# The same steps in a new written order on all five engines of a one-core macaron block with routed experts

## What is computed

```python
x = x + 0.5 * quantized_ffn(layernorm(x))          # int8 activations and weights
x = x + rg_lru_layer(layernorm(x))                 # conv, gated scan, then a gelu MLP of 512
x = x + 0.5 * quantized_ffn(layernorm(x))
x = x + 0.5 * moe(layernorm(x))                    # shared expert + top 2 of 8, inner width 256
x = x + gated_linear_attention(layernorm(x))       # state 128x128 for each of 16 sequences
x = x + 0.5 * moe(layernorm(x))                    # same weights again
```

## Time and profile before

| | |
|---|---|
| runs | 701.73, 701.86, 702.95 us; median 701.86 |
| profiled execution, its span | 703.3 us |
| PE / PEld busy | 616.8 us (88%) / 487.0 us (69%) |
| DVE busy | 487.2 us (69%) |
| ACT busy | 398.0 us (57%) |
| POOL busy | 387.9 us (55%) |
| moved by DMA | 100.99 MB, mean 144 GB/s |

### The profile page before, as it was taken

The page is one execution under the profiler, slowest core; times in us unless marked ns, Lnnn a source line. Parts: engine busy times, 40 slices in busy tenths (PEclk is TensorE's granted clock), DMA queues, the critical chain, the costliest instruction groups (busy, mean ns, idle before and its releaser), DMA issues.

```text
span 703.3 us, 14597 instructions
## 1 busy us (share of the span) xinstructions
PE 616.8 (88%) x4232; PEld 487.0 (69%) x4232; DVE 487.2 (69%) x1730; ACT 398.0 (57%) x1036; POOL 387.9 (55%) x416
## 2 busy tenths in 40 slices
PE   1478999999799989899986998899999999987971
PEld 1234565566566888788885886779878998776970
DVE  6986777878889867554625996878865874546334
ACT  3477887999686454554445556464665446343530
POOL 4425434435747787767653413651865764766642
PEclk9699999999999999999999999999999999999996
DMA  7998000000042366577668010214324545566886
GB/s 263 410 411 342 1 0 1 1 1 20 31 107 61 95 179 179 168 214 223 189 200 286 22 66 11 63 46 117 89 73 134 157 115 161 166 197 175 251 302 214
DMA packets 60126, 100.99 MB, mean 144 GB/s; under 512 B 10288, under 2 KB 28592, under 8 KB 59792
## 3 DMA queue, kind: packets, MB, share of 16 engines
q1 hardware_dynamic: 50832, 81.52, 37.7%
q0 software_dynamic: 8640, 17.84, 7.1%
q10 hardware_dynamic: 576, 0.69, 0.3%
HBM read 61.79 MB, written 38.23 MB: 142 GB/s over the span
## 4 chain that ended last, share of the span: by engine, by line
PE 59%; DVE 10%; ACT 9%; issue 7%; DMA 6%; POOL 5%; SPq 4%; POOLq 0%; ACTq 0%; DVEq 0%
PE bank L1071 14%; PE bank L1048 7%; PE bank L1282 4%; PE bank L934 3%; DMA tin<-rows_by_expert 3%; PE bank L959 3%; PE bank L308 3%; PE bank L945 3%; PE bank L510 3%; PE bank L663 3%; PE bank L313 3%; POOL rows_by_expert L830 2%; PE bank L677 2%; PE bank L1054 2%; PE bank L692 2%
## 5 line engine op out<-in xcount | busy, mean ns | idle before, releaser
L830 POOL DMA_INDIRECT rows_by_expert<-xx,sidx x128 | 126.3, 987 | 71.7 <-DVE xx L809 35.8
L1071 PE MATMUL bank<-tint,twt 128*128 128x128 f32 x1136 | 150.7, 278 | 10.9 <-DVE thidt L1109 5.7
L1071 PEld LDWEIGHTS bank<-tint,twt 128*128 128x128 f32 x1136 | 138.6, 192 | 26.3 <-issue 13.6
L1109 DVE TENSOR_TENSOR thidt<-tsil,bank 128x256 f32<-128x256 f32 x142 | 58.9, 419 | 98.6 <-ACT tsil L1087 86.6
L1120 POOL DMA_INDIRECT rows_done<-tout,tin x98 | 95.4, 974 | 52.4 <-ACT tout L1095 28.3
L1087 ACT ACTIVATE tsil<-bank 128x256 f32<-128x256 f32 x142 | 54.4, 384 | 82.1 <-PE bank L1071 80.4
L1048 PE MATMUL bank<-e_dn,thidt 128*128 x568 | 89.8, 283 | 7.3 <-issue 3.5
L1048 PEld LDWEIGHTS bank<-e_dn,thidt 128*128 128x128 f32 x568 | 76.4, 193 | 19.4 <-issue 18.8
L1095 ACT ACTIVATE tout<-bank,tin 128x128 f32<-128x128 f32 x142 | 51.5, 367 | 35.1 <-PE bank L1054 33.7
L1120 POOL DMA_INDIRECT rows_done<-tout,tdst x44 | 43.8, 996 | 30.1 <-issue 11.8
L1080 ACT ACTIVATE tint<-bank 128x128 f32<-128x128 f32 x142 | 38.2, 275 | 37.1 <-PE bank L1054 36.8
(11 more groups left out here) (271 smaller groups left out, 1363.9 us busy)
## 6 DMA issues: line engine op xcount, KB each, us to landing
twt<-moe_gu SPq DMA_DIRECT2D x142, 256.0 KB
rows_by_expert<-tout SPq DMA_DIRECT2D x25, 715.0 KB, 19.6
tin<-rows_by_expert SPq DMA_DIRECT2D x142, 65.0 KB
hid<-rows_done SPq DMA_DIRECT2D x12, 512.0 KB, 4.8
x<-x_in SPq DMA_DIRECT2D x8, 256.0 KB, 4.1
rows_by_expert<-xx,sidx POOLq DMA_INDIRECT x128
out<-x SPq DMA_DIRECT2D x8, 256.0 KB, 3.5
rows_done<-tout,tin POOLq DMA_INDIRECT x98, 3.0
```

Of the source, the lines that this page charges most:

```text
L830: pool.indirect_dma_start(out=rows_by_expert, out_offset=bass.IndirectOffsetOnAxis(ap=sidx[h][:, k:k + 1], axis=0), in_=xx[h][:, r, t, :], ...
L1071: m = pe.matmul(bank[UP_BANKS[p][j]][:, c * P:(c + 1) * P], weights[:, c * P:(c + 1) * P], tint[g % TURNS][:, :], start=True, stop=True)
L1109: dve.tensor_tensor(thidt[g % TURNS][:, :, :].rearrange("p j c -> p (j c)"), tsil[g % TURNS][:, :], bank[UP_BANKS[p][j]][:, INNER:2 * INNE ...
```

## The change

Steps, semaphores, waits inside the steps and buffers are the same. Each of the five lists holds the same steps as before, in another order. Counted by index in their list, 246 of 315 steps of SyncE, 504 of 637 of VectorE, 158 of 285 of GpSimd, 564 of 711 of TensorE and 622 of 751 of ScalarE stand at another place, by at most 7, 41, 22, 19 and 26 places. The order of some is turned around between neighbours; loops are written anew for it. The parts that matter here:

```diff
@@ -1476,277 +1476,216 @@
         @block.sync
         def _(sp_):
             k_loads_sync(sp_)
-            for j in range(0, 2):
+            for j in range(0, 9):
                 t_load_sync(sp_, 0, j)
...
+            t_load_sync(sp_, 0, 63)
+            for j in range(61, 63):
+                t_weights_sync(sp_, 0, j)
             t_stored_sync(sp_, 0, 0)
             c_fetch_sync(sp_, 0, 0)
             c_fetch_sync(sp_, 1, 0)
-            t_load_sync(sp_, 0, 66)
-            for j in range(63, 65):
+            for j in range(64, 67):
+                t_load_sync(sp_, 0, j)
+            for j in range(63, 67):
                 t_weights_sync(sp_, 0, j)
-            for j in range(67, 70):
+            t_load_sync(sp_, 0, 67)
+            c_fetch_sync(sp_, 2, 0)
+            t_weights_sync(sp_, 0, 67)
+            for j in range(68, 70):
                 t_load_sync(sp_, 0, j)
-            c_fetch_sync(sp_, 2, 0)
-            t_weights_sync(sp_, 0, 65)
             c_fetch_sync(sp_, 3, 0)
-            for j in range(66, 70):
+            c_fetch_sync(sp_, 4, 0)
+            for j in range(68, 70):
                 t_weights_sync(sp_, 0, j)
-            c_fetch_sync(sp_, 4, 0)
+            t_load_sync(sp_, 0, 70)
             t_weights_sync(sp_, 0, 70)
-            t_load_sync(sp_, 0, 70)
...
+            for j in range(66, 69):
+                t_load_sync(sp_, 1, j)
+            t_weights_sync(sp_, 1, 66)
             t_stored_sync(sp_, 1, 0)
             c_fetch_sync(sp_, 0, 1)
-            t_load_sync(sp_, 1, 67)
-            for j in range(65, 67):
+            t_weights_sync(sp_, 1, 67)
+            for j in range(69, 71):
+                t_load_sync(sp_, 1, j)
+            for j in range(68, 70):
                 t_weights_sync(sp_, 1, j)
-            t_load_sync(sp_, 1, 68)
             c_fetch_sync(sp_, 1, 1)
-            t_load_sync(sp_, 1, 69)
-            for j in range(67, 69):
-                t_weights_sync(sp_, 1, j)
-            t_load_sync(sp_, 1, 70)
             c_fetch_sync(sp_, 2, 1)
-            t_weights_sync(sp_, 1, 69)
-            c_fetch_sync(sp_, 3, 1)
             t_weights_sync(sp_, 1, 70)
             o_store_sync(sp_, 0)
+            o_store_sync(sp_, 1)
+            c_fetch_sync(sp_, 3, 1)
             c_fetch_sync(sp_, 4, 1)
-            o_store_sync(sp_, 1)
-            o_store_sync(sp_, 2)
             c_fetch_sync(sp_, 5, 1)
             t_stored_sync(sp_, 1, 6)
             c_fetch_sync(sp_, 6, 1)
+            o_store_sync(sp_, 2)
+            o_store_sync(sp_, 3)
             t_stored_sync(sp_, 1, 7)
             c_fetch_sync(sp_, 7, 1)
-            o_store_sync(sp_, 3)
...
 
         @block.vector
         def _(dve):
+            q_stats_vector(dve, 0, 0)
             q_limits_vector(dve, 0, 0)
-            q_stats_vector(dve, 0, 0)
             q_mom1_vector(dve, 0)
+            q_limits_vector(dve, 1, 0)
             k_first_vector(dve)
+            q_stats_vector(dve, 1, 0)
+            q_mom1_vector(dve, 1)
             q_par1_vector(dve, 0)
-            q_stats_vector(dve, 1, 0)
             q_scale_vector(dve, 0, 0)
-            q_limits_vector(dve, 1, 0)
             q_whole_vector(dve, 0, 0)
-            q_mom1_vector(dve, 1)
             q_par1_vector(dve, 1)
             q_scale_vector(dve, 1, 0)
+            q_whole_vector(dve, 1, 0)
             q_out_vector(dve, 0, 0)
-            q_whole_vector(dve, 1, 0)
-            q_limits_vector(dve, 2, 0)
+            q_stats_vector(dve, 3, 0)
+            q_stats_vector(dve, 2, 0)
             f_stats_vector(dve, 0)
-            k_weights_vector(dve)
             q_out_vector(dve, 1, 0)
             f_stats_vector(dve, 1)
             f_mom_vector(dve, 0)
+            k_weights_vector(dve)
+            k_decay_vector(dve)
+            q_limits_vector(dve, 2, 0)
             q_limits_vector(dve, 3, 0)
-            q_stats_vector(dve, 2, 0)
-            q_stats_vector(dve, 3, 0)
             q_mom_vector(dve, 1, 0)
             q_limits_vector(dve, 4, 0)
             q_par_vector(dve, 1, 0)
             q_scale_vector(dve, 2, 0)
+            q_scale_vector(dve, 3, 0)
             q_whole_vector(dve, 2, 0)
+            q_whole_vector(dve, 3, 0)
+            q_stats_vector(dve, 4, 0)
             q_limits_vector(dve, 5, 0)
-            q_stats_vector(dve, 4, 0)
             q_stats_vector(dve, 5, 0)
-            q_limits_vector(dve, 6, 0)
             q_mom_vector(dve, 2, 0)
-            k_decay_vector(dve)
-            q_stats_vector(dve, 6, 0)
-            q_scale_vector(dve, 3, 0)
-            q_whole_vector(dve, 3, 0)
-            q_limits_vector(dve, 7, 0)
             q_out_vector(dve, 2, 0)
+            f_stats_vector(dve, 2)
             q_par_vector(dve, 2, 0)
+            q_scale_vector(dve, 4, 0)
             f_left_vector(dve, 0)
+            q_whole_vector(dve, 4, 0)
             f_ix_vector(dve, 0)
-            f_stats_vector(dve, 2)
-            q_scale_vector(dve, 4, 0)
-            f_ix_vector(dve, 1)
+            q_out_vector(dve, 3, 0)
             f_left_vector(dve, 1)
-            q_out_vector(dve, 3, 0)
             f_stats_vector(dve, 3)
             f_mom_vector(dve, 1)
             f_scan_vector(dve, 0)
             f_hy_vector(dve, 0)
             f_apply_vector(dve, 0)
...
+            q_whole_vector(dve, 5, 1)
+            q_stats_vector(dve, 6, 1)
+            r_slot_vector(dve, 2, 0)
+            q_out_vector(dve, 4, 1)
             e_add_vector(dve, 1, 0)
-            m_add_vector(dve, 6)
-            r_slot_vector(dve, 2, 0)
-            q_whole_vector(dve, 5, 1)
-            q_out_vector(dve, 4, 1)
...
             x_hid_vector(dve, 0, 4)
+            q_par_vector(dve, 3, 1)
+            q_scale_vector(dve, 6, 1)
+            q_whole_vector(dve, 6, 1)
+            x_hid_vector(dve, 0, 5)
             r_bias_vector(dve, 4, 0)
+            q_scale_vector(dve, 7, 1)
             e_hid_vector(dve, 3, 0, 0)
             r_rank_vector(dve, 4, 0)
-            x_hid_vector(dve, 0, 5)
+            x_hid_vector(dve, 0, 6)
             r_slot_vector(dve, 4, 0)
-            q_par_vector(dve, 3, 1)
-            x_hid_vector(dve, 0, 6)
-            q_scale_vector(dve, 6, 1)
-            q_whole_vector(dve, 6, 1)
-            x_hid_vector(dve, 0, 7)
-            q_scale_vector(dve, 7, 1)
+            q_whole_vector(dve, 7, 1)
             e_hid_vector(dve, 3, 0, 1)
...
@@ -2298,18 +2222,19 @@
             x_hid_vector(dve, 1, 30)
             r_slot_vector(dve, 6, 1)
             x_hid_vector(dve, 1, 31)
+            table_vector(dve, 1, 3)
+            x_hid_vector(dve, 1, 32)
             e_hid_vector(dve, 6, 1, 0)
-            for j in range(32, 34):
+            for j in range(33, 35):
                 x_hid_vector(dve, 1, j)
             e_hid_vector(dve, 6, 1, 1)
-            x_hid_vector(dve, 1, 34)
-            table_vector(dve, 1, 3)
             x_hid_vector(dve, 1, 35)
             e_add_vector(dve, 6, 1)
             for j in range(36, 38):
                 x_hid_vector(dve, 1, j)
+            taken_vector(dve, 1, 3)
+            x_hid_vector(dve, 1, 38)
             r_bias_vector(dve, 7, 1)
...
-            for j in range(62, 64):
+            for j in range(59, 64):
                 x_hid_vector(dve, 1, j)
-            e_add_vector(dve, 7, 1)
-            x_dst_vector(dve, 1, 64)
-            x_hid_vector(dve, 1, 64)
+            for j in range(64, 66):
+                x_dst_vector(dve, 1, j)
+            for j in range(64, 66):
+                x_hid_vector(dve, 1, j)
+            for j in range(66, 68):
+                x_dst_vector(dve, 1, j)
+            x_hid_vector(dve, 1, 66)
+            for j in range(68, 70):
+                x_dst_vector(dve, 1, j)
             c_add_vector(dve, 0, 1)
-            x_hid_vector(dve, 1, 65)
-            x_dst_vector(dve, 1, 65)
-            x_hid_vector(dve, 1, 66)
-            for j in range(66, 69):
-                x_dst_vector(dve, 1, j)
-            for j in range(67, 69):
+            c_add_vector(dve, 1, 1)
+            x_dst_vector(dve, 1, 70)
+            for j in range(67, 71):
                 x_hid_vector(dve, 1, j)
-            c_add_vector(dve, 1, 1)
-            x_hid_vector(dve, 1, 69)
-            x_dst_vector(dve, 1, 69)
-            x_hid_vector(dve, 1, 70)
             c_add_vector(dve, 2, 1)
-            x_dst_vector(dve, 1, 70)
             c_add_vector(dve, 3, 1)
             c_add_vector(dve, 4, 1)
             c_add_vector(dve, 5, 1)
             c_add_vector(dve, 6, 1)
+            e_add_vector(dve, 7, 1)
             c_add_vector(dve, 7, 1)
...
+            q_root_gpsimd(pool, 3, 1)
+            r_scatter_gpsimd(pool, 3, 0, 3)
             t_store_gpsimd(pool, 0, 0)
-            r_scatter_gpsimd(pool, 3, 0, 2)
-            r_scatter_gpsimd(pool, 3, 0, 3)
-            q_root_gpsimd(pool, 3, 1)
+            q_bias_gpsimd(pool, 6, 1)
+            q_bias_gpsimd(pool, 7, 1)
             for j in range(1, 4):
```

(71 more changed lines are left out.)

2498 lines of the change are left out of this document (1185 added, 1313 removed).

## The result

The changed kernel took 716.16 us (median of 711.69, 715.06, 717.26 and 718.38), the kernel before 702.4 us in the same measurement (its three runs of above and one of 708.17): a ratio of 1.0162, 95% interval 1.0106 to 1.0218. It is slower by 1.6%, where I forecast 695.4 us and put 0.15 on slower. Measured again beside later experiments the ratio was 1.0181 [1.013, 1.0231].

A forecast was written before the change was run, and what follows sets the result against it. No single engine was taken to bound the kernel; four stages have different limits. Terms -4.2 + 2.7 + 0.8 - 0.5 - 5.3 = -6.5 us gave 695.4 us at the median (from 701.86), range 685.5 to 702.5.

The forecast's parts named there:

- Start, -4.2 us: First units up to m_gate(0,0): it starts at 61.5 instead of 65.74 us, and the full stage after carries the gain.
- The 0.9 us that I counted for the clock: Start, 55.1 to 58.5 us: with shorter idle times part of 2.81 us of TensorE work runs at 2.4 GHz.
- `q_turn(4)`: Start: its wait for q_out(3) counted at 1.25 us; holding TensorE by more than 3 us would show the prediction wrong.
- Tables: ScalarE's table loads fall from 36 to 31, 6.4 us less of ScalarE; nothing added to the sum for it.
- the term of +2.7 us: GpSimd's stage, 214 to 334 us: gives back 2.7 of the 4.2 us through VectorE delaying r_slot(2,0), q_bias and r_root(3,0).
- slower rival: Middle stage: late q_scale(7,1) or r_mom(3,0) holds GpSimd, 15.0 us in all, giving 707.7 us; chance 0.15.
- Switch, +0.8 us: Switch to the attention, 364 to 384 us: two more row loads ahead of tile 63's weights cost 0.8 us.
- Units 6 and 7, -0.5 us: Second pass: an earlier table(1,3) wins 1.7 us at e_add(6,1) and loses 1.2 us ahead of it.
- The end, -5.3 us: 640 to 703 us: four pieces of TensorE's time before the last store go, 1.62 + 1.79 + 1.13 + 0.79 us.
- my bound at 0: End: nothing is won if the read-backs that c_add(0,1) and c_add(1,1) wait for land 5 us later than thought.
- the 680 that I had named as a sign of being wrong: End: the prediction is wrong if c_add(1,1) starts past 680 us on the new scale.
- no change: Rival: the end gives nothing and the sum is -1.2 us, 700.7 us, or the start is eaten too; chance 0.08.

The follow-up runs named there:

- e1: All five lists in the new order up to 214 us, the old order from there; 700.0 us against 705.12 for the kernel before, ratio 0.9936.
- e5: Old kernel with all five lists in the new order between 214 and 370 us only; ratio 1.0109 [1.0067, 1.015] to the kernel before.
- e13: Old kernel with the new order between 370 and 650 us only, four g_bias in a row; 710.8 us against 706.42, ratio 1.0074.
- e4: Old order up to 640 us, new order from there; 708.27 us against 705.12 for the kernel before, ratio 1.0034.
- e6: Changed kernel with the stretch from 214 to 364 us in the old order; 817.76 us, ratio 0.9963 [0.992, 1.0007] to the kernel before.
- e8: Changed kernel with 214 to 364 us in the old order and the four g_bias steps apart; 815.37 us, ratio 0.9912 to the kernel before.
- e14: Old kernel with the new order between 370 and 650 us only, g_bias steps taken apart; 706.63 us against 706.42, ratio 1.0014.
- e16: The changed kernel itself, unaltered, measured and traced again; 718.89 us against 706.42 for the kernel before, ratio 1.0181 [1.013, 1.0231].
- e12: New order up to 214 us, old behind, with f_si(1) moved on ScalarE directly behind f_square(1); ratio 0.9893 [0.9803, 0.9983] to the kernel before.
- e9: Old kernel with the new order between 214 and 300 us only; ratio 1.0083 [1.0043, 1.0122] to the kernel before.
- e17: Changed kernel with SyncE's whole list in the old order; 730.06 us against 705.57 for the kernel before, ratio 1.0341.
- e18: Changed kernel with x_up(40), x_up(41), the last wave's table and tile 24's weights put back; 715.2 us, ratio 1.0128 to the kernel before.
- e3: Old kernel with only g_bias of units 0, 1 and 2 side by side on GpSimd; 709.59 us against 705.12, ratio 1.0075.
- e2: Changed kernel with only the four g_bias steps taken apart on GpSimd; 714.55 us against 705.12 for the kernel before, ratio 1.0147.
- e7: Old kernel with two end moves: tile 65's weights ahead of t_stored(1,0), and e_down(7,1) last with e_add(7,1) just before c_add(7,1); ratio 0.9993.
- e11: Old order up to 640 us, new end, but c_add(0,1) and c_add(1,1) behind VectorE's products of tiles 67 to 70; ratio 1.0081 to the kernel before.

## Why the prediction was wrong, step by step

**The ledger.** Each stage's new order alone in the old kernel: start -0.64% (e1), 214 to 370 us +1.09% (e5), 370 to 650 us +0.74% (e13), end +0.34% (e4). The sum is +1.53%; the whole change measured +1.62% and +1.81%. So this sum comes out, but it is no proof: each share has an interval of 0.3 to 0.4% to both sides, e5's comes from a series at 821 us, and leaving stages out does not give the same. By the sum e6 (all but the middle) should be at +0.44% and e8 (the same without the row, e14's share) at -0.16%; they measured -0.37% [-0.8, +0.07] and -0.88% [-1.28, -0.47]. Taken out of the new kernel the middle is worth some 2%, put into the old one 1.1%. My sum had -4.2, +3.5 (2.7 + 0.8), -0.5 and -5.3 us for them; at 702 us measured shares make -4.5, +7.7, +5.2 and +2.4 us.

**Start, -4.2 us: the size was right, its way only in part.** `m_gate(0,0)` came at 62.92, -2.8 us, not 61.5, and in e1 and e16, with the same order, at -1.5 and -1.4. The rest of the lead was won between there and `r_slot(2,0)`, in the stage in which I had said that nothing can be won; that the total fits is partly luck. `f_b(0)` came at 49.01, where I placed it at 48.3 behind a shorter wait for ScalarE, and `f_mix(0)` at 53.77 instead of 52.2. The 0.9 us that I counted for the clock did not come: it was low for 3.4 us again (51.8 to 55.2), and TensorE was busy for 3.29 us of them instead of 2.81. I had no term for `f_si(1)`, which ScalarE now runs behind two table loads and for which `f_y(1)` waits 2.70 us. By e12 that wait is not the cause of the rest: without it `f_mix(0)` waits 4.19 us for VectorE. At `r_slot(2,0)` the kernel was 4.4 us earlier (3.3 in e1), and e1 keeps -0.64%. `q_turn(4)` held nothing.

**Tables: right.** 31 loads, nothing gained or lost elsewhere by it that can be seen.

**"The 85 transfers are the same and stay back to back, so this stage can shift but hardly shrink": the first step that failed.** It is the term of +2.7 us in my sum, and the stage cost 5.3 us at its last scatter and some 7.7 us by the ledger. (The tiles from 49 on are the fifth wave, not the fourth as I wrote.) `q_bias(7,1)` waited 0.94 us, as forecast, and `r_root(3,0)` not at all. Waits ending at another engine were 8.1 us in the two groups (I said some 8; 5.7 before), but that is luck: the increase is the stores' wait for ScalarE, 5.7 us after 3.2, which I had not named. The slower rival's mechanism, GpSimd held by 15 us at two steps, did not happen either. Yet the lead of 4.4 us became 0.9 us late at the last scatter, and 7.8 us late at `x_up(57)`: GpSimd was not what counted alone. From 214 to 334 us TensorE works 5.2 us less than in the earlier trace rows, in waits of up to 1.7 us each, the longest in front of steps of tiles 19, 24, 25 and 42; behind that stage one of 1.46 us stands in front of tile 50. In all, TensorE is idle for 15.3 us between `x_up(0)` and `x_up(57)` instead of 7.5, and 3.4 us more are at the low clock. The weights of tile 24 are issued behind the rows of five later tiles, and `x_hid(17)` stands behind `r_rank(6,0)`. At 307.50 even a store starts 3.88 us late, behind ScalarE, with a scatter queued behind it. I had priced two waits on GpSimd and taken TensorE's stage as covered because it "looks busy"; at 114 of 120 us it was just as full as GpSimd with the gaps between its transfers (111.6), and the loss was not given back. e5 shows the place (1.1%), and e9 points to its part before 300 us (0.8%). That it is a sum of many such waits rather than one is what the trace suggests and what e17 and e18 are in keeping with, but no run shows it; which list starts it **stays open**: of the five, only SyncE's was put back alone, and that made it worse.

**Switch, +0.8 us: did not come.** `x_up(63)` had 0.41 us of idle time in front of it, not 4.5; a wait of 2.35 us for rows stood earlier, at 378.35. The clock was low for 6.9 us there (379.5 to 386.4) instead of 3.4, and yet `g_level(0,0)` was 1.4 us less late than `x_up(57)`.

**Not in the sum at all: the row of four `g_bias` on GpSimd.** I wrote that "no instruction is added or removed apart from table loads, so every term is a wait made shorter or longer", and went on to price the list order by waits at semaphores only. Here an instruction itself became 5.4 us longer. It is the largest loss whose cause is shown: about 6 us at its place (e6 against e8, e13's trace), 4.2 us at the end (e13 against e14), 4.5 us when put into the old kernel (e3). In the changed kernel itself its share of the time stays open (e2). It was visible ahead. In the timeline of the kernel before, `g_bias(0)` on GpSimd lies over a VectorE instruction of 1.80 us whose like took 0.69 us just before; I hadn't set the two side by side. First GpSimd, then VectorE:

```profile
386.60 1.28 POOL L1182 TENSOR_TENSOR x<-x,rows 128x512 f32<-128x512 f32 x1
```
```profile
384.41 0.69 DVE L1150 TENSOR_TENSOR x<-x,hid 128x512 f32<-128x512 f32 x1
...
386.63 1.80 DVE L1150 TENSOR_TENSOR x<-x,hid 128x512 f32<-128x512 f32 x1
```

**Units 6 and 7, -0.5 us: too small to be seen** (e14: 1.0014 [0.9984, 1.0044] for the whole of 370 to 650 us without the row).

**The end, -5.3 us: the second step that failed; nothing was won.** The moves did to TensorE what I said: no wait before `x_up(65)`, `e_down(7,1)` last, `c_add(7,1)` 8.97 us behind the last store (9.1 forecast). But I added four pieces of TensorE's time as if the last store followed from their sum. In e4 the last store is as late as `x_up(49)` of the second pass (+6.4 both), and in the changed kernel it wins 1.1 us on it (+11.2, +10.1 at the store) but loses 2.4 us when traced again (e16). Between `x_up(65)` and the last store the eight traces with the new end take 15.2 to 17.5 us (mean 16.3), ten with the old end 13.8 to 15.4 us (mean 14.7; e7 and e17, which mix the two, left out), so there the new end costs time. What was won comes back as waits between `x_up(65)` and the store: rows of tiles 69 and 70, ScalarE, and `x_hid(67)` at 693.83 behind the sums `c_add(0,1)` and `c_add(1,1)`, which waited for their read-back (1.88 us at 692.36; `x_up(67)` was done at 692.05). That last one was my bound at 0, but e11 shows that it is not the cause by itself: with the sums late the end is no faster. The two moves of e7 held 3.4 us of my sum, a ratio of 0.995; they gave 0.9993, and 0.995 is just outside its interval. `c_add(1,1)` started at 692.36; `x_up(49)` was 11.2 us late where I had expected 1.2 us early, and with these 12.4 us taken off it is 679.9, just at the 680 that I had named as a sign of being wrong.

**The range and the chances.** The upper end, 702.5, was my own "no change" plus a little. The slower rival had the right stage, the wrong mechanism and its decision point (10.6 us on GpSimd) far from what was needed, because the losses ran through other engines as well: TensorE's waits, an instruction of VectorE, the end. An order rewritten in hundreds of places, which I said I "can't sum", was given a cost of nothing with bounds only for a gain ("if those win another 4 us"); the same ignorance should have stood on the slower side.

**The best version** is e1, the new order up to 214 us and the old from there: 700.0 against 705.12 us, 0.6% less than the kernel before (the changed one, in other series, is 1.6 and 1.8% above it).

## What to carry to other kernels

A stage in which two engines are both taken up for over nine tenths (here TensorE by its work, GpSimd by its transfers and the gaps between them) has no cover: price every reordered step on both, and if there are too many, keep an equal bound on the slow side. When steps of GpSimd move, look at what VectorE does at the same moment, since an instruction there can be stretched even where no semaphore ties the two; keep long GpSimd operations apart, and out of a chain of VectorE and TensorE. Pieces of idle time that vanish ahead of a last store are gains only up to the next thing that the store waits for; test an order by stage and keep the stages that win.

## What the runs showed of the hardware

- A VectorE operation of 0.28 us became 5.67 us beside four elementwise instructions of GpSimd on 128x512 in a row (1.23 us each), one of 0.43 us became 4.28 beside three, and beside one GpSimd instruction one of 0.69 us became 1.80 and one of about 0.16 us became 1.08 (e14). Each had two inputs and ended within 0.6 us behind the last GpSimd instruction. In all seven traces with three or four in a row VectorE did not get a turn between them; the one beside four took 5.67 or 5.68 us in each of six. Eight VectorE statistics with one input kept their 0.28 us beside such an instruction (e14).
- With 4.98 us without a matmul TensorE's clock fell to 1.2 GHz for 6.9 us (410.2 to 417.1), with 3.78 us in e3 as well (410.0 to 416.8), but with 4.98 us in e13 for 3.4 us (405.6 to 409.0). Other such stretches in the changed kernel lasted 3.4 us (51.8 to 55.2, 328.3 to 331.7, 464.8 to 468.2).
- In two of the five series the same kernel before took 821 us instead of 705. e7 is such a run, and its order until the end is that of the kernel before. In its trace ScalarE is idle for 107.5 us and VectorE for 41.5 us in waits whose releaser the profile can't name ("remote"); the trace of before has no such wait. TensorE's clock is low 18 times instead of 5. Two groups of ScalarE in e7 (in before 82.1 and 37.1 us of idle time):

```profile
L1087 ACT ACTIVATE tsil<-bank 128x256 f32<-128x256 f32 x142 | 54.4, 385 | 133.3 <-PE bank L1071 66.7 <-remote 50.4 <-issue 13.9
L1080 ACT ACTIVATE tint<-bank 128x128 f32<-128x128 f32 x142 | 38.3, 276 | 50.3 <-PE bank L1054 25.3 <-remote 20.3 <-issue 4.4
```

The series of e13 to e16, at 706 us, ran on the same chip as that of e5 to e8, so it is not the chip. What causes it, and whether the clock is a cause or follows, no run here shows.
